# A routed feed-forward pair in a 12-sublayer decoder: the second weight matrix of all eight experts kept in SBUF and picked by a register on TensorE, instead of being loaded with every tile

## The reference, cut to what matters

```python
# first sublayer: the two best of 8 experts per token (softmax over their two logits)
y = sum_r weight_r * (gelu_tanh(x @ w1[e_r] + b1[e_r]) @ w2[e_r] + b2[e_r])
# last sublayer: the best of 8 experts, up to a capacity of 1281 tokens per expert
h = gelu(x @ W1[e] + b1[e]);  y = (h @ W2[e] + b2[e]) * score     # 0 beyond the capacity
```

## Time and profile before

| | |
|---|---|
| median of 3 runs | 3676.05 us (3666.92 to 3680.37) |
| span of the profiled execution | 3676.0 us |
| TensorE busy, weight loads busy | 2923.5 us (80%), 2031.9 us (55%) |
| VectorE, ScalarE, GpSimd busy | 2180.6, 1827.8, 1827.1 us |
| DMA moved | 315.46 MB, mean 86 GB/s |
| expert loads | 85 + 53 of 578.0 KB |
| mean granted TensorE clock | 0.891 of 2.4 GHz |

### The profile page before, as it was taken

The page is one execution under the profiler, slowest core; times in us unless marked ns, Lnnn a source line. Parts: engine busy times, 40 slices in busy tenths (PEclk is TensorE's granted clock), DMA queues, the critical chain, the costliest instruction groups (busy, mean ns, idle before and its releaser), DMA issues. The chain is left out here.

```text
span 3676.0 us, 83888 instructions
## 1 busy us (share of the span) xinstructions
PE 2923.5 (80%) x28814; PEld 2031.9 (55%) x28814; DVE 2180.6 (59%) x5986; ACT 1827.8 (50%) x3516; POOL 1827.1 (50%) x1735
## 2 busy tenths in 40 slices
PE   2778867897888699954529997996999869995884
PEld 2667755574555456642416664664445536664774
DVE  2111134657888578862347886777898677884125
ACT  0333334744555466621216665775466677662442
POOL 3542354535777655526465554664033655553425
PEclk9999988899999799975559998998999889996997
DMA  8566652020101121114621112221000012222764
GB/s 289 181 186 187 187 150 76 22 5 25 41 37 43 44 75 68 65 47 129 167 52 43 57 54 88 87 86 54 1 1 1 1 30 63 72 64 91 213 209 143
DMA packets 325161, 315.46 MB, mean 86 GB/s; under 512 B 111348, under 2 KB 244886, under 8 KB 324505
## 3 DMA queue, kind: packets, MB, share of 16 engines
q1 hardware_dynamic: 283240, 261.98, 23.5%
q0 software_dynamic: 16384, 33.59, 3.0%
q10 hardware_dynamic: 25264, 16.40, 1.5%
HBM read 167.28 MB, written 60.69 MB: 62 GB/s over the span
## 5 line engine op out<-in xcount | busy, mean ns | idle before, releaser
L936 DVE TENSOR_TENSOR moe_first_tile_y<-moe_first_out_ps,moe_first_expert_w 128x256 f32<-128x256 f32 x85 | 35.7, 423 | 372.5 <-PE moe_first_out_ps L1067 180.3
L1056 PE MATMUL moe_first_hid_ps<-moe_first_tile_xT,moe_first_expert_w 128*128 128x256 f32 x680 | 182.5, 415 | 42.3 <-ACT moe_first_hid L1118 39.9
L1067 PE MATMUL moe_first_out_ps<-moe_first_expert_w,moe_first_hid 128*128 128x128 f32 x1360 | 173.6, 281 | 11.4 <-issue 10.3
L1067 PEld LDWEIGHTS moe_first_out_ps<-moe_first_expert_w,moe_first_hid 128*128 128x128 f32 x1360 | 172.5, 197 | 17.2 <-issue 11.6
L1137 POOL DMA_INDIRECT slot_x<-x_tok,moe_first_slots x128 | 123.9, 968 | 110.1 <-DVE moe_first_slots L908 48.6
L1118 ACT ACTIVATE moe_first_hid<-moe_first_hid_ps,moe_first_expert_w 128x256 f32<-128x256 f32 x340 | 138.2, 473 | 68.8 <-PE moe_first_hid_ps L1056 43.2
L794 POOL DMA_INDIRECT moe_first_token_y<-slot_y,moe_first_slots x128 | 123.8, 967 | 95.8 <-issue 67.7
L1056 PEld LDWEIGHTS moe_first_hid_ps<-moe_first_tile_xT,moe_first_expert_w 128*128 128x128 f32 x680 | 135.0, 210 | 65.2 <-issue 45.0
L1870 POOL TENSOR_TENSOR causal_k_blocks<-causal_k_T,headmask 128x1024 f32<-128x1024 f32 x64 | 121.3, 1898 | 99.6 <-PE causal_scores L1480 94.0
L1870 POOL TENSOR_TENSOR alibi_k_blocks<-alibi_k_T,headmask 128x1024 f32<-128x1024 f32 x64 | 121.3, 1896 | 94.1 <-PE alibi_scores L1480 90.0
L1870 POOL TENSOR_TENSOR full_k_blocks<-full_k_T,headmask 128x1024 f32<-128x1024 f32 x64 | 120.7, 1896 | 84.2 <-PE full_scores L1480 79.2
(11 more groups left out here) (561 smaller groups left out, 9047.8 us busy)
## 6 DMA issues: line engine op xcount, KB each, us to landing
moe_first_expert_w<-in_L_attn_experts SPq DMA_DIRECT2D x85, 578.0 KB
moe_last_expert_w<-in_L_ffn_experts SPq DMA_DIRECT2D x53, 578.0 KB
moe_first_tile_x<-slot_x SPq DMA_DIRECT2D x85, 128.0 KB
slot_y<-moe_first_tile_y SPq DMA_DIRECT2D x85, 128.0 KB
slot_x<-blank ACTq DMA_DIRECT2D x2, 4992.0 KB
L_ffn_tile_x<-slot_x SPq DMA_DIRECT2D x32, 256.0 KB
slot_y<-L_ffn_tile_y SPq DMA_DIRECT2D x32, 256.0 KB
moe_last_tile_x<-slot_x SPq DMA_DIRECT2D x53, 128.0 KB
```

The costliest lines, as they stand in the source:

```text
L936: dve.tensor_tensor(y_out[:, q, :, :], out_bank[q][:, 0:SLOT_TILE].rearrange("p (s d) -> p s d", s=SPAN), over(wall[:, j % RING, 2 * FF + ...
L1056: last = pe.matmul(hid_bank[h][:, SLOT_TILE * (b % 2):SLOT_TILE * (b % 2) + SLOT_TILE], wall[:, j % RING, 128 * b:128 * b + 128], xT[:, j ...
L1067: last = pe.matmul(out_bank[j % 2][:, D * s:D * s + D], hid[:, j % 2, b, TILE * s:TILE * s + TILE], wall[:, j % RING, FF + D * b:FF + D * ...
```

## The change

The second matrices of all eight experts are loaded once per routed sublayer, by one DMA of 2 MB into a tile `downs`, placed in SyncE's program before the first expert loads. The load of each tile brings the rest (644 columns, 322 KB). The packed row is reordered so that this rest stands first. TensorE reads the number of the tile's expert into a register before `output(j)` and uses it in the address of the moving operand of its eight products; before the first one it waits for `downs`. At the first tile of a part it waits for `planned` too. The biases keep their place in the ring with new offsets.

```diff
-        wall = sb("expert_w", [128, RING, W])
+        wall = sb("expert_w", [128, RING, RW])            # RW = FF + FB + D
+        downs = sb("expert_down", [128, E, FB * D])
...
                 net.next_weights(sp)
-                own = sp.alloc_register(f"{name}_expert")
+                sp.dma_start(downs[:, :, :], experts[:, :, RW:].rearrange("e p w -> p e w")).then_inc(downs_landed, 16)
...
                     sp.dma_start(wall[:, j % RING:j % RING + 1, :].rearrange("p o w -> p (o w)"),
-                                 experts[bass.ds(e, 1), :, :].rearrange("o p w -> p (o w)"))\
+                                 experts[bass.ds(e, 1), :, 0:RW].rearrange("o p w -> p (o w)"))\
...
+                def expert_of_tile(j):
+                    part, n = tile_of[j]
+                    if n == 0:
+                        pe.wait_ge(planned, 2 * part + 1)
+                    return pe.value_load(expert_of[0:1, part, n:n + 1], min_val=0, max_val=E - 1)
+
                 def output(j):
+                    if j == 0:
+                        pe.wait_ge(downs_landed, 16)
+                    e = expert_of_tile(j)
                     if j >= 2:
                         pe.wait_ge(out_done, j - 1)
...
                             last = pe.matmul(out_bank[j % 2][:, D * s:D * s + D], hid[:, j % 2, b, TILE * s:TILE * s + TILE],
-                                             wall[:, j % RING, FF + D * b:FF + D * b + D], start=(b == 0), stop=(b == FB - 1))
+                                             downs[:, bass.ds(e, 1), D * b:D * b + D].rearrange("p o d -> p (o d)"),
+                                             start=(b == 0), stop=(b == FB - 1))
...
         arrays[f"{layer}_experts"] = np.concatenate(
-            [up, down..., up_b..., np.broadcast_to(down_b...)], axis=2)
+            [up, up_b..., np.broadcast_to(down_b...), down...], axis=2)
```

13 lines of the change are left out of this document (7 added, 6 removed).

## The result

The changed kernel takes 3684.09 us (median of 20 runs), the kernel before 3674.90 (median of 20 runs beside them). The ratio is 1.0025, 95% interval 1.0018 to 1.0033: the change makes the kernel slower by 9 us, with an interval of 7 to 12. The forecast was faster by 16 us. One of the changed kernel's 20 runs took 4071.64 us at a granted clock of 0.711; it is left out of the ratio.

The account below looks back on a forecast made before the run. The prediction took TensorE as the busiest engine in the tile stages, with 211 of 726 us delay, partly waits for rows and GpSimd's bursts. Its terms: 3676 - 24 + 6 + 2 = 3660 us, range 3636 to 3728 us.

Parts of the forecast that it names:

- -24 us for the smaller loads: Tile stages of moe_first and moe_last: expert loads of 322 instead of 578 KB shorten TensorE's waits for rows, -24 us.
- I count two waits in three: Of TensorE's waits for a tile's rows, 25 shrink by 0.9 us each, 22 us, plus 2 us for short waits.
- 37 waits: TensorE's waits for the load of a tile's rows in both tile stages, 77.5 us in total before the change.
- The lower bound of 0: Smaller loads gain nothing if every wait for rows is for a load issued late, after a late VectorE eviction.
- +6 us for the read and the addresses: TensorE's register read and register-addressed products before each output: mostly hidden behind the array, +6 us, lower bound 0, upper 166 us.
- about 20 tiles of that kind: Tiles where TensorE's sequencer leads the array by only 0.9 us, so the output's dispatch ends 0.3 us late.
- +2 us for the 2 MB load: Start of moe_first: the 2 MB load may hold up routing, +2 us, at most 5.5; in moe_last 0.
- The signs in the profile: Tile stages: DMA share down about 0.15, waits for rows 77.5 to about 50 us, undelayed tiles 3.73 us, output's matmuls unchanged.
- Dispatch binds: TensorE's sequencer takes twice the price per register-operand matmul, every tile 1.2 us longer: 3764 us, halfway 3709; chance 0.28.
- The gain goes into the bursts: Earlier tiles only meet GpSimd's bursts earlier and evictions wait for their end; the 24 us are lost: 3684 us; chance 0.14.
- The larger gain: Smaller loads also free the DMA engines for scatters and gathers, and all 37 waits shrink: 3643 us; chance 0.10.

## Why the prediction was wrong

**Direction.** Forecast 3660, measured 3684: 16 us faster was said, 9 slower came. The measured time lies in the range that was given (3636 to 3728). Of the 25 us between the two, 18 are the first of the terms below and 7 the second.

**-24 us for the smaller loads: mis-sized, 5 to 6 us.** The step that failed is "I count two waits in three". It rested on the chain of one execution, four of whose five loads of rows took over 3.3 us. Two measurements contradict it. A load of rows takes 2.71 and 2.73 us on the mean from issue to landing in moe_first in the two traces of the kernel before, 2.58 and 2.51 in those of the changed kernel; in moe_last 2.78 and 2.75 against 2.55 and 2.67. It lands about 0.17 us earlier, not 0.9. 37 waits x 0.17 = 6 us, of the size that was measured, though that measurement is too coarse to confirm it. And without nearly all expert loads a load of rows still takes 2.47 and 2.37 us on the mean, and the waits in moe_first stay (44.4 against 47.7 us). The 0.9 us were the bytes' price at full flow, but the load of rows is issued 2.06 us behind the expert load, which by my own figure needs 2.1 us: it finds most of it done. (That this is the reason is argued; the 0.17 us are measured.) The lower bound of 0, "if all were of the late-issued kind", was nearer the truth, and the earlier trace rows had shown that kind.

**+6 us for the read and the addresses: too low, though each instruction was cheaper than taken.** Read and check take 0.59 us where 0.94 was taken, four register instructions of 0.046 us stand where the estimate had eight of 0.08 with their gaps, and undelayed tiles stay at 3.73 us, as forecast. The whole price with the 2 MB load is 15 us, not 8. The step that failed is the exposure: "about 20 tiles of that kind", 0.3 us each. I took the lead that the sequencer has in quiet tiles and asked only whether the output starts late. In quiet tiles it doesn't; but the middle part of moe_first, with its long bursts, alone loses 4 to 7 us after the loads' gain (203 to 207.3, 209.8, 207.6) and 10 to 12 without it. The forecast had no term for the granted clock, and most of what the read alone costs there is the same products at a lower one. That the read is the cause there is shown (207.8 with it alone, 225.1 with four, 204.1 without the reads). By which path 0.59 us on the sequencer become that is not shown: the read itself grows in a burst by 0.7 us at most (to 1.33 from its start to the end of its check).

**+2 us for the 2 MB load: not contradicted.** 1.0006 is 2 us, with an interval of 5 to each side; the first output ends 0.2 to 1.3 us later.

**The signs in the profile.** DMA share down by 0.11 and 0.13 (0.15 was said), waits for rows down to 62.6 us (50), undelayed tiles at 3.73 us, output's matmuls unchanged. They came about as steps of a gain, the waits for rows by about half, and the time went the other way. The waits of one engine for one cause aren't a ledger of the time. In the middle part TensorE's waits for rows fell from 21.3 us to 13.1, and those that no engine ended (issue) rose from 7.3 to 15.5. The first of the two is not even firm (in the middle part 16.6 and 21.7 us in two more executions without the change there, 20.2 and 19.2 in two with it); the second is (9.5 and 6.5 against 15.9 and 12.3). The rows of the changed kernel:

```profile
PE moe_first_turn_ps L1047 <- DMA moe_first_tile_x<-slot_x: 13.1, 7, 3.8
...
PE moe_first_out_ps L1078 <- issue: 7.4, 10, 1.7
PE moe_first_turn_ps L1047 <- issue: 5.2, 1, 5.2
PE moe_first_hid_ps L1058 <- issue: 2.9, 2, 1.6
```

**The rivals.** Dispatch binds (3764, halfway 3709): it doesn't with one read, as the 3.73 us show; with four it begins to. The Trainium skill (TensorE: Matmul & The Clock Gate, What happens when you issue a matmul) gives 62 ns for each matmul that the sequencer's ucode has to handle. Sixteen matmuls with register operands still follow one another in 1.95 us, 0.12 us each, so a price of that size would be hidden and no run here shows whether it is paid. Its other figure, a floor of about 600 ns for a register load (DMA: Bandwidth & Descriptors, Latency and other measured facts), is twice the 302 ns of the row; with the bounds check it comes to 590. The gain goes into the bursts (3684): this rival gave the measured time to the microsecond, by luck: its terms are others (0 and +8, where -5 to -6 and +15 were measured), and its sign in the profile, more than 169.2 us at evictions, didn't come (160.7). That GpSimd's DMAs take the gain is supported: with 144 of them gone the change pays 12 us. That the length of their runs does it is not: with the runs spread the change still loses. And GpSimd's own rate can be the last chain through the end of moe_last, which I hadn't seen. The larger gain (3643) is out: even without the loads it is 24 us.

## What to carry to other kernels

Before you price what a lighter transfer gives, take it away altogether in one run: that bounds the gain, and here the bound was the whole of what a cut by 44 per cent had been promised. Look at the chain of more than one execution, since a chain near a balance of two engines runs now through the one and now through the other. And a per-tile instruction on an in-order sequencer isn't free because ordinary tiles hide it: ask what it costs where the engine is already served late. Nor do prices measured one at a time add up there: two that were measured as 1 and 2 us alone came to 15 together.

## What the runs showed of the hardware

- During a run of GpSimd's indirect DMAs (1.25 us each) the other engines come to a near standstill (from 8 us on in the run shown) and go on 1 to 3 us after the last one. After the runs of 16 in moe_first an output is evicted up to 15.5 us after its end, after runs of 8 in its first 22 tiles up to 4.8. Fetching what 144 gathers had brought by plain DMAs of SyncE made the kernel 52 and 67 us faster, 0.4 us per gather. The cause isn't known. The Trainium skill (SBUF — State Buffer, Who interferes with whom) names a port that VectorE and GpSimd share; that can't be all of it, since ScalarE and TensorE stand as well.
- A register read on TensorE takes 302 ns and its bounds check brings it to 590; a moving operand addressed by a register costs one register instruction of 46 ns per distinct slice and, with one read per tile, no time on the array in an undelayed tile. Read and addresses together cost more than each alone.
- TensorE's granted clock in the middle part of moe_first is 0.92 in the kernel before, 0.90 in the changed one and 0.99 in the kernel before without the gathers. The same 1033 matmuls are busy for 161.3, 166.6 and 154.1 us, so pauses that go away give back more than their own length.
